# A fused retention, mixture and attention kernel: first normalizations of two sequences cut in two pieces, four fills of constant rows issued by ScalarE

## What is computed

```python
x = x + retention(layernorm(x))     # 2 layers, 16 heads of 8, decay per head, feed-forward 512, GELU
x = x + experts(layernorm(x))       # 8 experts, the best 2 of each token, SiLU gate, 512 hidden
x = x + attention(layernorm(x))     # causal softmax, 16 heads of 8
x = x + experts(layernorm(x))       # the same experts again
```

```python
def _layernorm(x, axis=-1, eps=1e-05):
    m = jnp.mean(x, axis=axis, keepdims=True)
    v = jnp.var(x, axis=axis, keepdims=True)
    return (x - m) / jnp.sqrt(v + eps)
```

## Time and profile before

| | |
|---|---|
| median of 3 runs | 858.31 us (856.56 to 863.74) |
| profiled execution | 862.67 us, span 860.9 us, mean granted clock 0.874 |
| PE busy | 646.4 us (75%) |
| VectorE busy | 593.6 us (69%) |
| ScalarE busy | 371.7 us (43%) |
| GpSimd busy | 288.5 us (34%) |

### The profile page before, as it was taken

One profiled execution on the slowest core, in us unless ns is written; L12 is line 12 of the kernel. 1 busy time (PEld: TensorE's weight loads), 2 busy tenths in 40 slices (PEclk: granted clock), 3 DMA queues, 4 the chain that ended last, 5 costly groups with the idle time before them and its releaser, 6 DMA issues.

```text
span 860.9 us, 19286 instructions
## 1 busy us (share of the span) xinstructions
PE 646.4 (75%) x6492; PEld 448.3 (52%) x6492; DVE 593.6 (69%) x1760; ACT 371.7 (43%) x642; POOL 288.5 (34%) x554
## 2 busy tenths in 40 slices
PE   2867999999794135999726779898899971699990
PEld 1434645666464125999712334444444531599990
DVE  2684689766977733888665786677778635487874
ACT  2436577565343211444232346565465641344430
POOL 0131365545332732555503000110413132246550
PEclk9887999999996557999955598999999995799995
DMA  9300991000000127555337122311322000355545
GB/s 301 128 1 2 198 200 30 2 2 2 1 8 19 62 68 167 147 163 170 112 111 179 31 49 57 81 44 42 106 58 55 2 26 16 105 162 154 168 140 152
DMA packets 98568, 75.75 MB, mean 88 GB/s; under 512 B 8060, under 2 KB 90812, under 8 KB 98332
## 3 DMA queue, kind: packets, MB, share of 16 engines
q1 hardware_dynamic: 92872, 63.10, 29.5%
q0 software_dynamic: 4544, 9.38, 3.2%
q10 hardware_dynamic: 1056, 2.04, 0.7%
HBM read 49.32 MB, written 23.20 MB: 84 GB/s over the span
## 4 chain that ended last, share of the span: by engine, by line
PE 56%; DVE 16%; issue 9%; DMA 7%; ACT 6%; POOL 3%; SPq 3%; DVEq 0%; ACTq 0%; POOLq 0%
PE PC L2107 7%; PE PA L2097 5%; PE PB L2097 5%; DVE rmax L1435 4%; PE P L2190 4%; PE PC L2010 4%; PE PA L2150 3%; PE P L2030 3%; PE PA L2148 3%; POOL rows_dram L778 3%; PE PA L1988 2%; PE P L2039 2%; DMA ffn_w<-in_w 2%; PE P L1912 2%; PE PC L2173 2%
## 5 line engine op out<-in xcount | busy, mean ns | idle before, releaser
L1435 DVE TENSOR_REDUCE rmax<-PA 128x1 f32<-128x512 f32 (+3 forms) x256 | 120.0, 488 | 50.4 <-PE PA L2150 43.7
L790 POOL DMA_INDIRECT outs_dram<-va,ids x78 | 81.0, 1039 | 105.4 <-DVE va L1371 97.6
L2107 PE MATMUL PC<-ffn_w,pm 128*128 128x128 f32 x624 | 88.1, 285 | 12.5 <-DMA ffn_w<-in_w 12.2
L2150 PE MATMUL PA<-kst,qst 96*128 96x512 bf16 (+3 forms) x256 | 84.4, 335 | 0.0
L2107 PEld LDWEIGHTS PC<-ffn_w,pm 128*128 128x128 f32 x624 | 76.9, 194 | 14.0 <-DMA ffn_w<-in_w 13.6
L1741 ACT ACTIVATE kv_b<-P 128x256 f16<-128x256 f16 x78 | 29.9, 383 | 121.6 <-PE P L2086 121.6
L2148 PE MATMUL PA<-mqb,idb 128*128 128x128 bf16 x256 | 60.6, 238 | 25.1 <-DVE rmax L1435 17.5
L1361 DVE SCALAR_TENSOR_TENSOR pm<-PB,invb,decay 128x512 f32<-128x512 f32 x78 | 58.5, 750 | 20.7 <-ACT decay L1749 12.8
L2148 PEld LDWEIGHTS PA<-mqb,idb 128*128 128x128 bf16 x256 | 25.5, 99 | 87.5 <-DVE rmax L1435 49.0
L2097 PE MATMUL PA<-kv_b,pm 128*128 128x128 f16 x936 | 68.1, 225 | 0.0
L2097 PE MATMUL PB<-kv_b,pm 128*128 128x128 f16 x936 | 66.9, 223 | 0.0
(11 more groups left out here) (271 smaller groups left out, 1475.6 us busy)
## 6 DMA issues: line engine op xcount, KB each, us to landing
ffn_w<-in_w SPq DMA_DIRECT2D x78, 256.0 KB
rows_dram<-wall SPq DMA_DIRECT2D x1, 8385.0 KB, 47.3
proj_w<-rows_dram SPq DMA_DIRECT2D x78, 65.0 KB, 1.9
qst<-parts_dram SPq DMA_DIRECT2D x48, 96.0 KB
kst<-parts_dram SPq DMA_DIRECT2D x48, 96.0 KB
parts_dram<-qkp SPq DMA_DIRECT2D x16, 256.0 KB, 2.7
qst<-in_w SPq DMA_DIRECT2D x8, 256.0 KB, 5.8
kst<-in_w SPq DMA_DIRECT2D x8, 256.0 KB, 7.0
```

The source lines that it names most:

```text
L790: nc.gpsimd.indirect_dma_start(out=outs_dram, out_offset=bass.IndirectOffsetOnAxis(ap=ids[:, k % YB:k % YB + 1], axis=0), in_=ysb[:, k % Y ...
L1435: nc.vector.tensor_reduce(rmax[:, i, h % HG:h % HG + 1], PA[:, n % 2, 0:(i + 1) * P], AX_X, ALU.max).then_inc(pair_sb[n % 2], 1)
L2107: ins = mm(PC[:, k % 2, 0:D], eT[:, k % 2, f, :], w2b[k % WB2][:, f, :], start=f == 0, stop=f == FB - 1)
L2150: mm(bank[:, 0:w], qst[0:KS, s % 2, o + i * P:o + w], kst[0:KS, s % 2, o:o + w], start=False, stop=True, skip_group_check=True).then_inc(p ...
```

## The change

`norm_twice` becomes `first_sums` (mean and variance) and `first_factors` (the rest, with the wait for `xn_ready`). Sequence 1 has both in step 0 as before. Sequence 2 has its sums in step 2 and its factors in step 3, sequence 3 its sums in step 5 and its factors in step 6. The five constants, with the wait for the fourth `xn_ready`, go from step 6 to step 7. The four transfers of constant rows are issued by ScalarE, one behind the gate of tile 2, 6, 10 and 14 each.

```diff
@@ SyncE @@
                 for n in range(NTL):
                     w2_load(n, expert[n])
                     if (m, n) == (0, 2):
-                        stack_constants()
                         sp.dma_start(bo[:, :], a_bo.partition_broadcast(P)).then_inc(in_att, 16)
                     if n + AHEAD < NTL:
                         expert.append(rows_in(n + AHEAD))
@@
-            def stack_constants():
-
-                sp.wait_ge(filled, 3)
-                for b in range(2):
-                    for stack, fill in ((qst, zeros), (kst, ones)):
-                        sp.dma_start(stack[KQ:KS, b, :].rearrange("r (h n) -> r h n", h=H),
-                                     fill.unsqueeze(1).to_broadcast([KS - KQ, H, L])).then_inc(stack_fill, 16)
@@ VectorE @@
-            def norm_twice(s):
-
-                if s >= 2:
-                    dve.wait_ge(xn_ready, s)
+            def first_sums(s):
+
                 for k in range(TPS):
                     ins = nc.vector.bn_stats(st6[:, k, :], X[:, TPS * s + k, :])
                 link(ins)
                 for k in range(TPS):
                     ins = nc.vector.bn_aggr(mv[:, k, :], st6[:, k, :])
                 link(ins)
+
+            def first_factors(s):
+
+                if s >= 2:
+                    dve.wait_ge(xn_ready, s)
                 nc.vector.tensor_scalar(rs[:, 0, 0:TPS], mv[:, 0:TPS, 1], EPS, None, ALU.add)
...
@@
-                norm_twice(0)
+                first_sums(0)
+                first_factors(0)
@@
-                    if t in (0, 3, 5):
-                        s = (0, 3, 5).index(t) + 1
+                    if t in (0, 2, 5):
+                        s = (0, 2, 5).index(t) + 1
                         dve.wait_ge(in_x[s], 16)
-                        norm_twice(s)
-                    if t == 6:
+                        first_sums(s)
+                    if t in (0, 3, 6):
+                        first_factors((0, 3, 6).index(t) + 1)
+                    if t == 7:
                         dve.wait_ge(xn_ready, SEQ)
@@ ScalarE @@
+            def stack_constants(i):
+
+                stack, fill = ((qst, zeros), (kst, ones))[i % 2]
+                if i == 0:
+                    act.wait_ge(filled, 3)
+                    act.wait_ge(rows_out, 16 * PICKS * NT)
+                    act.wait_ge(w_lo, E)
+                act.dma_start(stack[KQ:KS, i // 2, :].rearrange("r (h n) -> r h n", h=H),
+                              fill.unsqueeze(1).to_broadcast([KS - KQ, H, L])).then_inc(stack_fill, 16)
@@
                     gate(k)
+                    if m == 0 and k % 4 == 2 and k // 4 < 4:
+                        stack_constants(k // 4)
```

## The result

The changed kernel takes 850.84 us, the median of four runs (847.67 to 852.58). The kernel before, run beside it, has a median of 861.01 us (856.56 to 863.74, four runs with the three shown ahead of the prediction). The ratio is 0.9885, with a 95% interval of 0.985 to 0.9921. So it is faster by 9.9 us (6.8 to 12.9 by the interval). The forecast was 17.5 us and 840.8 us, within 836 to 849: the direction came out, the size did not.

What follows compares the result with a forecast made beforehand. It took TensorE to wait for a late VectorE in the blocks, and for weights held up by SyncE's fill issues in the experts. 6.0 + 11.5 = 17.5 us off the median 858.31 gave 840.8 us, range 836 to 849.

Steps and rivals of the forecast that it cites:

- Sums of sequence 2 cost nothing: VectorE, step 2: sums of 1.31 us fit 1.66 us of idle time; step 4 begins 1.3 us earlier.
- Factors of sequence 3 to step 6: VectorE, step 5: tile 6's keys and values come 2.46 us earlier; the 3.99 us pause shrinks to a little over 1 us.
- The 7.52 us go: VectorE, step 6: its idle time for `first_rows(3)` goes when the wait for the fourth `xn_ready` moves to step 7.
- term A: Blocks: gain from moving VectorE's sums, factors and constants, 6.0 us, within 3.5 to 7.0.
- ScalarE is late next: Behind step 7: TensorE's turn waits for ScalarE's unbroken row, comes at 71.9 to 75.5, pauses 5 to 6 us.
- Issue on ScalarE and SyncE free: Experts: fills cost ScalarE at most 0.1 us each; SyncE is past `bo` some 9 us earlier, tile 3's weights at about 324.0.
- Term B: First experts: gain from moving the four fills to ScalarE, 12.97 - 1.5 = 11.5 us, within 5 to 13.
- the price of the four fills on the weights behind them: First experts: fills hold back the next weights, 0 to 8 us for four, taken as 1.5 us.
- First rival, the transfers were the wait: Experts: each fill delays a needed load, TensorE pauses four times, some 2 us each; time 848 us; chance 0.15.

Runs made afterwards that it cites:

- Casts only: Changed kernel, but sums and factors of sequences 2 and 3 stay together at the old places; only the constants with their wait move to step 7; one run, 859.63 us.
- split only: Changed kernel, but the five constants with their wait for the fourth `xn_ready` stay at the end of step 6; one run, 851.22 us.
- norms only: Changed kernel's VectorE code, but SyncE issues the four fills in one go as before; 853.42 us, 0.9928 of the kernel before.
- spread-out fills on SyncE: Changed kernel, but SyncE issues the four fills, one each behind the second weights of tiles 2, 6, 10 and 14; 847.43 us, 0.9851 of the kernel before.
- kernel with halves: Changed kernel, but eight fills of 8 heads each, one behind the gate of every second tile from 2 to 16; 845.41 us, 0.9817 of the kernel before.
- Fills only: Changed kernel's fills on ScalarE, but the normalizations on VectorE as in the kernel before; 856.14 us, 0.995 of the kernel before.
- weight sums behind the turn: Changed kernel, but ScalarE's two weight sums (2.08 us) go behind the turn that TensorE waits for; 849.35 us, 0.9867 of the kernel before.
- fills elsewhere: Changed kernel, but SyncE issues three fills ahead of the first experts and one behind the last second weights; 843.60 us, 0.9787 of the kernel before.

## Why the prediction was right in its direction and wrong in its size

- *Sums of sequence 2 cost nothing:* right. They went into the idle time ahead of tile 3's keys and values, and tile 4's come 1.33 us earlier (predicted 1.3).
- *Factors of sequence 3 to step 6:* right. Tile 6's keys and values came at 57.50, between 57.3 and 58.8, and the pause before the projection is 1.45 us ("a little over 1 us").
- *"The 7.52 us go":* the wait went, but it was worth nothing by itself. Casts only was 1.3 us or more slower in the block stretch than the old code, split only as good as the whole. So term A came out with one of its three parts worth nothing.
- *ScalarE is late next:* right, at 73.78 within 71.9 to 75.5, with a pause of 5.93 us ("5 to 6") and half clock behind it; step 8 takes 7.69 us against 5.98, 1.7 us lost where 1.6 were counted. The weight sums moved off that row gave 2.1 us.
- *Term A, 6.0 us within 3.5 to 7.0:* held. The block stretch gives 5.0 us in the pair of profiles and 5.3 between means; norms only, timed, 6.2.
- *Issue on ScalarE and SyncE free:* right in what was said of the issues, though spreading alone would have freed SyncE as well. Fills of 0.79 to 1.45 us; tile 3's weights issued at 318.94, 15.4 us earlier, where 324.0 less the shift of 5.9 was said (318.1).
- *Term B, 11.5 us within 5 to 13:* **the step that failed** is the price of the four fills on the weights behind them, "for four, 0 to 8 us; I take 1.5, nearer to the row that was measured". They cost 5.6 us by the pauses, 5.3 by the run without fills in the stretch. So the term was 12.97 - 5.6 = 7.4, and the stretch shows 6.7 to 7.1.
  The row chosen was the wrong one: tile 2's weights, with no pause "beside two fills", were issued at 322.32, *ahead* of the fill at 322.75. In the changed kernel the fill goes out first, 1.22 and 0.59 us ahead of the weights (317.72 and 318.94, 329.19 and 329.78), and those take 5.6 to 6.0 us for a lead of 4.1 and 4.8 us. The spread-out fills on SyncE bear the reading out: there the weights issued 0.43 us ahead of each fill brought no pause. It is no full rule, for in the kernel with halves weights issued 0.9 us ahead of a piece took 4.88 us. The prediction had written that each later fill comes "within 0.2 us of the next weights", and that its upper bound was the fill's own 3 us, "of which perhaps 2 reach TensorE"; 1.0 to 1.9 did. With the upper bound's reading the sum would have been about 11.
- *First rival, the transfers were the wait:* half right. Each fill does make TensorE pause, but by 1.4 us on average, since the weights' lead absorbs the rest. The 3 us that the prediction reckoned for a fill fit what it adds to the landing (5.5 to 6.0 less 3.0 us). Its time of 848 us was nearer to 850.84 than the forecast.
- *What remains:* the two stretches gain 5.0 + 7.1 = 12.1 us in the pair of profiles and 5.3 + 6.7 = 12.0 between the means, the times 9.9 (6.8 to 12.9 by the interval). In the first pair of profiles the executions differ by 15.0 us, in the second by 3.8 (855.64 and 851.86). Behind the stretches, from attention on, the three profiles with the old code have 393.8 to 397.9 us and the changed kernel's two 395.2 and 397.7. Whether some 2 us are given back there or all is chance was not settled. Fills only points the same way: 7.2 us in its stretch, 4.3 timed, just beyond the interval of 1.7 to 7.0.

The range of 836 to 849 missed by 1.8 us. Had the fills' price been left between 0 and 8 and the value taken in its middle, the forecast would have been 843; with the weights' place behind the fill read rightly, 845 to 847. Part of the rest is the baseline: the three runs of the kernel before that were shown have a median of 858.31, the four beside the changed kernel 861.01, and 859.95 to 860.72 in three later comparisons, so it stood some 2 us low. The other part are the 2 us between stretches and times, which stay open.

## What to carry to other kernels

When a long transfer is moved next to a short one that is needed soon, look which of the two is issued first: that a load ahead of it was in time tells little of a load behind it. What it costs is the load's landing time behind it less the lead that the load has (here 5.5 to 6.0 us against 4.1 to 4.8). So cutting it into pieces whose extra time fits into the lead hides most of it, two in a row cost more than two apart, and putting it where nothing is due costs nothing; which engine issues it changed how the pause came about but not the sum. And when a wait is taken off one engine, price what is late next from that engine's unbroken row before moving anything else: here moving the casts' wait brought nothing, the split all.

## What was not expected of the hardware

- A 256 KB load that landed in about 3.0 us with no fill about took 5.4 to 6.5 us when it was issued within 1.3 us behind a fill of 384 KB to 24 partitions on the other queue (changed kernel twice, fills only, weight sums behind the turn); in the changed kernel's first profile the DMA share was 0.86 to 0.99 meanwhile. Behind a fill on its own queue it was issued later and landed in 3.5 to 4.3 us, at 0.76 to 0.80. Both ways TensorE lost about the same.
- The issue of a fill costs 0.79 to 1.45 us alone, but the third in a row 2.2 us. So it was in the first experts (2.18 in the earlier trace rows) and also ahead of them, where only the loads of `wqkv` and `wo` went before. SyncE in the kernel with the fills elsewhere:

```profile
278.67 1.08 SPq L655 DMA_DIRECT2D kst<-vs  x1
279.80 0.78 SPq L655 DMA_DIRECT2D qst<-vs  x1
280.63 2.23 SPq L655 DMA_DIRECT2D kst<-vs  x1
```

- The same program is granted 0.50 or 1.00 of TensorE's clock in step 2 from one execution to the next, which moves all behind it by 2.9 us (39.45 and 36.58). Step 6 of the kernels with both norm edits takes either 7.74 or 9.3 us, with norms only and the changed kernel on either side. So a difference of 3 us between two single profiles of this kernel means nothing until it is placed in a stretch.
